# Loading the convolution's stacks in twelve transfers a half image instead of six, in a shifted-window attention and graph-convolution kernel

## The reference

```python
# block 0
xn = layernorm(x over channels); xs = roll(xn, (-4, -4)); windows of 8 x 8
attn = softmax(q k^T * scale + bias + mask); out = proj(attn v); roll back
x = shortcut + out
y = layernorm(x.transpose(0, 2, 3, 1).reshape(B, H * W, C))
y = y.reshape(B, C, H, W)          # the memory of (token, channel), read as (channel, row, column)
y = einsum('oc,bchw->bohw', pin_w, y)
y = conv 3x3 depthwise, zero borders, of y
y = gelu(y[:, :h]) * y[:, h:]
x = x + einsum('oc,bchw->bohw', pout_w, y)
# block 1: 1x1 convolution and norm, column and row minima of shifted differences, two 1x1
# convolutions with gelu, a residual, and a two-layer MLP
```

## Time and profile before

| | |
|---|---|
| median of three runs | 233.95 us (233.3 to 235.31) |
| the profiled execution, its own time | 234.66 us |
| span of the profiled execution | 232.9 us |
| mean granted TensorE clock | 0.983 |
| PE, DVE, ACT, POOL busy | 91%, 68%, 59%, 55% of the span |
| DMA queue of SP | 11606 packets, 23.16 MB |

### The profile page before, as it was taken

One profiled execution on the slowest core, in us unless ns is written; L12 is line 12 of the kernel. 1 busy time (PEld: TensorE's weight loads), 2 busy tenths in 40 slices (PEclk: granted clock), 3 DMA queues, 4 the chain that ended last, 5 costly groups with the idle time before them and its releaser, 6 DMA issues.

```text
span 232.9 us, 8582 instructions
## 1 busy us (share of the span) xinstructions
PE 211.2 (91%) x3634; PEld 110.3 (47%) x3634; DVE 159.1 (68%) x282; ACT 136.9 (59%) x226; POOL 127.1 (55%) x164
## 2 busy tenths in 40 slices
PE   7759899999999999978899999997999958999970
PEld 4327666676758676656554444443333312222230
DVE  4587969698998989795756765334378688755321
ACT  3547676777868696843344343333266665989870
POOL 8245948476969879693989982224210000336342
PEclk9999999999999999997999999999999999999996
DMA  5950000220121462564536378677400001344212
GB/s 172 291 140 3 3 3 6 43 67 3 48 63 41 121 251 68 197 218 149 198 102 247 117 222 216 214 213 243 160 3 0 4 3 34 76 104 101 62 37 68
DMA packets 12540, 25.09 MB, mean 108 GB/s; under 512 B 6617, under 2 KB 8161, under 8 KB 10774
## 3 DMA queue, kind: packets, MB, share of 16 engines
q1 hardware_dynamic: 11606, 23.16, 33.0%
q0 software_dynamic: 896, 1.38, 2.7%
HBM read 18.63 MB, written 3.15 MB: 94 GB/s over the span
## 4 chain that ended last, share of the span: by engine, by line
PE 82%; DVE 7%; issue 4%; POOL 2%; ACT 2%; DMA 1%; POOLq 0%; DVEq 0%
PE psum L657 13%; PE psum L658 12%; PE psum L602 10%; PE psum L613 7%; PE psum L631 6%; PE psum L846 4%; PE psum L562 4%; PE psum L648 3%; PE psum L558 3%; PE psum L826 3%; PE psum L804 3%; PE psum L817 2%; PE psum L569 2%; PE psum L585 2%; PE psum L742 2%
## 5 line engine op out<-in xcount | busy, mean ns | idle before, releaser
L501 POOL TENSOR_TENSOR diff<-biased,mx 128x768 f32<-128x768 f32 x32 | 47.2, 1475 | 24.7 <-DVE mx L1133 23.6
L1129 DVE TENSOR_TENSOR biased<-psum,pk 128x768 f32<-128x768 f32 x32 | 30.5, 953 | 13.2 <-PE psum L602 13.0
L1248 DVE TENSOR_TENSOR gated<-psum,gel 64x512 f32<-64x512 f32 x32 | 22.1, 694 | 25.2 <-ACT gel L1017 25.1
L320 POOL DMA_DIRECT2D out<-yo x28 | 14.3, 517 | 44.6 <-DVE yo L1350 44.6
L1017 ACT ACTIVATE gel<-psum 64x512 f32<-64x512 f32 x32 | 18.9, 592 | 31.3 <-PE psum L658 31.3
L941 ACT ACTIVATE pt<-psum 128x768 f32<-128x768 f32 x32 | 25.9, 809 | 17.1 <-PE psum L613 16.9
L657 PE MATMUL psum<-sta,pk 108*128 108x512 f32 x64 | 33.7, 608 | 1.2 <-issue 1.2
L658 PE MATMUL psum<-stb,pk 108*128 108x512 f32 x64 | 32.7, 592 | 0.0
L1133 DVE TENSOR_REDUCE mx<-biased 128x12 f32<-128x768 f32 x32 | 30.5, 953 | 1.1
L602 PE MATMUL psum<-kmv,stq 32*64 32x192 f32 x512 | 28.8, 340 | 1.0 <-DVE kmv L1235 1.0
L631 PEld LDWEIGHTS psum<-val,pt 128*32 128x32 f32 x1536 | 17.3, 112 | 11.6 <-issue 10.8
(11 more groups left out here) (105 smaller groups left out, 339.4 us busy)
## 6 DMA issues: line engine op xcount, KB each, us to landing
sta<-scratch SPq DMA_DIRECT2D x24, 288.0 KB
stb<-scratch SPq DMA_DIRECT2D x24, 288.0 KB
xtok<-xt SPq DMA_DIRECT2D x8, 192.0 KB, 4.3
xin<-xw SPq DMA_DIRECT2D x8, 192.0 KB, 5.5
x<-x1s SPq DMA_DIRECT2D x28, 48.0 KB
out<-yo POOLq DMA_DIRECT2D x28, 48.0 KB, 2.0
pk<-pack SPq DMA_DIRECT2D x1, 827.5 KB, 7.4
scratch<-ytok SPq DMA_DIRECT2D x4, 192.0 KB, 5.0
```

The costliest lines, as they stand in the source:

```text
L501: g.tensor_tensor(diff[:, t % 2].rearrange("q g w n -> q (g w) n"), scores_of, mx[:, t % 2].unsqueeze(2).to_broadcast([128, 4 * NH, WT]), ...
L1129: v.tensor_tensor(biased[:, slot].rearrange("q (p s) -> q p s", p=2), banks, wt("rpb").unsqueeze(1).to_broadcast([128, 2, 2 * NH * WT]), A ...
L1248: v.tensor_tensor(gated[64 * (b % 2):64 * (b % 2) + 64, b // 2, c * CH:(c + 1) * CH], bank(u % 4)[64:128], gel[:, u % 4, :], ALU.mult).the ...
```

## The change

`load_stack` goes over quarters of an image inside a half: for each of two quarters, each stack and each row offset one transfer, twelve a half. A transfer still fills 36 partitions, now with rows of 1024 floats (4 KB), 144 KB in all. The bytes are the same, the transfers twice as many: 96 instead of 48. The count that `edges` waits for goes from 48 to 96. The unused argument `paced` goes. Line numbers behind the function are two lower in the changed kernel (L298 becomes L295).

```diff
-        def load_stack(queue, b, h, paced=False):
-
-            half = NT // 2
-            for n in range(2):
-                c0, c1 = STACKS[n]
-                for y in range(3):
-                    if paced and (n or y):
-                        at, before = divmod(3 * n + y - 1, 3)
-                        queue.wait_ge(stack_in[at][b][h], 16 * (before + 1))
-                    src = scratch[b]
-                    off = PAD + (y - 1) * W - 1 + c0 * NT + half * h
-                    src = bass.AP(src.tensor, src.offset + off, [[NT, c1 - c0], [1, 3], [half // 2, 2], [1, half // 2]])
-                    dst = stack(n, b)[y:RS:3, half * h:half * h + half].rearrange("p (q n) -> p q n", q=2)
-                    queue.dma_start(dst, src).then_inc(stack_in[n][b][h], 16)
+        def load_stack(queue, b, h):
+
+            quarter = NT // 4
+            for q in (2 * h, 2 * h + 1):
+                for n in range(2):
+                    c0, c1 = STACKS[n]
+                    for y in range(3):
+                        src = scratch[b]
+                        off = PAD + (y - 1) * W - 1 + c0 * NT + quarter * q
+                        src = bass.AP(src.tensor, src.offset + off, [[NT, c1 - c0], [1, 3], [1, quarter]])
+                        queue.dma_start(stack(n, b)[y:RS:3, quarter * q:quarter * q + quarter], src)\
+                            .then_inc(stack_in[n][b][h], 16)
...
-                    pool.wait_ge(stack_in[n][b][h], 48)
+                    pool.wait_ge(stack_in[n][b][h], 96)
```

More of the change, by code:

```diff
@@ L394, in _ @@
                     wait_for_y(b)
-                    load_stack(sp, b, 0, False)
+                    load_stack(sp, b, 0)
                 if m in (5, 7):
-                    load_stack(sp, m // 2 - 2, 1, False)
+                    load_stack(sp, m // 2 - 2, 1)
             store_y(sp, 5)
```

## The result

The changed kernel takes 256.18 us, the median of four runs (254.36 to 257.43), against 234.44 us of the kernel before in the same comparison (233.3 to 235.31). The ratio is 1.0946, with a 95% interval of 1.089 to 1.1003: 21.7 us slower. The profiled execution took 257.43 us, with a span of 255.6 us and a mean granted clock of 0.938. The forecast was 249.9 us, with a range of 241 to 257.

What follows compares the result with a forecast made beforehand. Loads already end on the path at image 3, limited by movement; the split makes SP's issues the longer. 234.66 + 14.2 + 1.7 = 250.6 us profiled, 0.7 above the median: 249.9 us, range 241 to 257.

Steps and rivals of the forecast that it cites:

- the upper end: On SP's queue: y lands in 6.9 us, (1,0) starts 2.6 later and (2,0) another 3.9: 256.4 us.
- (a): SP's load issues: 48 more, each 0.797 us with the gap whatever the row's length, 4.78 us more a half.
- rival of the cheap issue: SP's load issues get cheap with the shorter row, 0.36 us each: 234 us, 233 to 236; chance 0.11.
- the partly cheaper one: SP's load issues get cheaper by a part, 0.70 us with the gap: 241 us, 236 to 246; chance 0.08.
- (b): SP's queue of loads and stores: longer halves push the start of (3,0) to 164.8, was 149.07.
- sign for a late y: On SP's queue: (1,0) far behind 109 or (2,0) behind 138 would show that y lands late.
- (c): On PE: conv(24) starts at 177.1 instead of 162.93, +14.2 us; (3,1) stays hidden by 0.8 us.
- (d): PE's clock around its pauses: slower convolutions behind the second pause cost +1.7 us, bounds 0 and 3.4.
- (e): The rest: two-part pattern, dropped argument, higher wait count, last row of `sta` and smaller packets, all costed at nothing.

Runs made afterwards that it cites:

- y(5) first, quarters: The changed kernel with the store of y(5) issued ahead of the load of (1,1) instead of behind it: 252.63 us, ratio 1.0693.

## Why the prediction held, and where its size was off

The sign and the mechanism were right, and the time, 256.18 us, lies at the upper edge of the range. That it still lies inside is in part luck: the upper end stood for y landing after 6.9 us, and no y took longer than 3.9 in the profiled execution; the time came near it by other delays. The profiled execution took 257.4 us against a sum of 250.6, 6.8 us more.

- **(a)** An issue of 0.797 us with the gap, whatever the row's length: right, shown with rows of 2, 4 and 8 KB. The rule from the Trainium skill that was weighed there ("DMA: Bandwidth & Descriptors", "Issuing engines are not separate DMA queues") didn't hold at this size: 0.746 us of issue stand against 0.61 us of movement. The rival of the cheap issue falls with it, and the rival of the partly cheaper one too.
- **(b)** The ledger of SP. Its steps gave (3,0) at 164.8; it came at 169.62. Of the 4.8 us, 3.2 are the late start of (0,0), in a stage with a lower clock that no load had touched. 1.6 came between (0,1) and (1,0): the ledger had all issues at the median, and the slow ones cost 1.0 inside (0,1) (97.85 to 108.49, up to 1526 ns for one) and 0.6 in the stores behind it. 0.9 came from y(5), which landed 3.90 us after its issue instead of 3.0 (the row of 137.25 against that of 141.20). 0.9 was given back in blocks of stores that shrank. From (2,0) on each block took what the ledger said, within 0.2 us. The prediction's sign for a late y, (1,0) far behind 109 or (2,0) behind 138, came up (113.36 and 141.20) with y only 0.9 us late: it was set in absolute times and couldn't tell a late start from a late landing.
- **(c)** From the start of the last issue of (3,0) to conv(24) I had 2.2 us of landing and 1.4 of masks, 3.6. It was 4.5: the landing took 3.1 us instead of 2.2. Together with the 4.8 this makes conv(24) 5.75 us later than forecast (182.85 against 177.1). Before conv(24) 2.5 us are idle, not 4 to 6: the convolutions at the lower clock filled the gap. That image 3's second half is hidden was right.
- **(d)** The clock. From conv(24) to conv(28) 12.08 us passed instead of 10.39, with a mean granted clock of 0.72 in the window of 182 to 188. That is 1.69 us, against 1.7 forecast. So close a match is partly luck: the pause ahead was 2.5 us and not 4 to 6, and the same stretch took 12.78 us behind a pause of 3.95 (quarters in images 2 and 3) and 13.27 behind one of 3.19 (y(5) first, quarters). Around conv(20) the clock was 0.55 over ten us and cost nothing at the end, as said.
- **(e)** At nothing, right for the masks and the count. The masks of (1,1) came at 142.28, 6.8 us later than before and not 2, and PE still didn't wait for them. One cover was thinner than the text had it: residual(7) waited 2.68 us for `x1s`, as x1(5)'s store stood behind a longer queue. PE still had to wait for image 2 behind it (0.85 us before conv(16)), so it didn't reach the end.
- From conv(28) to the end passed 1.1 us more than before, on code that is the same.

So the term that was mis-sized is the delay at conv(24): 14.2 us in the text, 19.9 in the trace. 3.2 of the difference belong to the execution, and the other 2.5 to three prices that were taken at the median or near the lower end of their rows (the slow issues, y(5)'s landing, the last landing), less what the stores gave back.

Against the medians the sum is short by nearly as much: they rose by 21.7 us, where it says 16.0. Only one of the four executions was profiled, so how much of those 5.7 us is a late start stays open.

## What to carry to other kernels

A load from DRAM costs SP's queue a nearly fixed time, here 0.70 to 0.75 us for 12 to 36 rows of 2 to 8 KB. Before splitting transfers, set that issue time beside the time the bytes take to move (here 0.75 against 1.2 us before the split, 0.61 after), and look at what stands behind them on the same queue. Where the issue becomes the longer of the two, the queue loses its slack, every later item moves by what the slack doesn't cover, and the sum arrives at the last awaited load. Where nothing behind is awaited soon and the movement still sets the landing, the split is nearly free (0.4% with image 3 alone). Moving issues to another engine puts them in front of that engine's own work, and the landings can get later, so cost both.

## What the runs showed of the hardware that was not expected

- An issue of 12 rows takes 0.700 us and one of 36 rows 0.746: a third of the rows saves 6%.
- POOL issues the same load in 0.572 us, less than SP. But with both queues at work the loads' landings took up to 6.5 and 9.0 us (quarters) and 19.1 us (halves). On SP alone the last row of (3,0) took 3.1 us with quarters, and the last row of (3,1) 10.5 us with halves (issued at 157.8, masks at 168.27 in the kernel before).
- The mean granted clock of the first 30 us differs from run to run (0.73 to 1.00 in windows of ten us), in code that is the same; where it is lower, the loads start later, by up to 3.2 us. The executions of the kernel before alone spread from 231.8 to 238.7 us. Effects below 1% can't be read from one profile.
